# Selective-scan block on one core: B and C spread by DMA, z and output products in array tiles, eight state buffers, and a new order of all steps

## The reference

```
x = x + L0(groupnorm(x))        # nearest of 256 words by cosine, mixed in where close
xn = layernorm(groupnorm(x)) * g + b          # over 256 channels
for each of 4 chunks of 64 channels:          # a "sequence" of 1024 steps
    xi, z = in_proj(chunk)                    # 128 + 128 rows
    xc = silu(causal_conv4(xi) + conv_b)
    dt, B, C = x_proj(xc)                     # 4, 16, 16 rows
    dt = softplus(dt_proj(dt) + dt_proj_b)
    h[d,s] = exp(dt[d]*A[d,s]) * h[d,s] + dt[d]*xc[d]*B[s]    # recurrence over L
    y[d] = sum_s h[d,s]*C[s] + D[d]*xc[d]
    y = out_proj(y * silu(z)) + skip * chunk
x = x + proj(layernorm(all four y))
```

## Time and profile before

| | us |
|---|---|
| three runs: median (lowest, highest) | 5035.2 (5031.6, 5037.42) |
| profiled execution, device time | 5045.31 |
| its span, first to last instruction | 5043.5 |
| busy: PE / DVE / ACT / POOL | 4261.0 / 4235.7 / 2601.2 / 3470.8 |
[...]

### The profile page before, as it was taken

The page is one execution under the profiler, slowest core; times in us unless marked ns, Lnnn a source line. Parts: engine busy times, 40 slices in busy tenths (PEclk is TensorE's granted clock), DMA queues, the critical chain, the costliest instruction groups (busy, mean ns, idle before and its releaser), DMA issues. The chain is left out here.

```text
span 5043.5 us, 50728 instructions
## 1 busy us (share of the span) xinstructions
PE 4261.0 (84%) x13584; PEld 1366.9 (27%) x13584; DVE 4235.7 (84%) x3517; ACT 2601.2 (52%) x3272; POOL 3470.8 (69%) x2101
## 2 busy tenths in 40 slices
PE   3888988888888888988888888888888889888887
PEld 2222323222232222322223232222322223222221
DVE  2688888888888889888888888888888898888886
ACT  2455555554555455455555555555454554555542
POOL 2667767667677766767667676676777667676664
PEclk8798888888898898988888888888988989888887
DMA  1446454554645546455554645546455464555543
GB/s 45 121 131 160 123 141 123 150 145 123 155 117 150 136 128 166 117 142 130 148 150 119 151 112 150 146 125 155 111 152 136 128 166 116 142 130 148 146 129 99
DMA packets 193349, 676.10 MB, mean 134 GB/s; under 512 B 23192, under 2 KB 25056, under 8 KB 189024
## 3 DMA queue, kind: packets, MB, share of 16 engines
q1 hardware_dynamic: 193120, 673.10, 51.7%
HBM read 572.34 MB, written 67.11 MB: 127 GB/s over the span
## 5 line engine op out<-in xcount | busy, mean ns | idle before, releaser
L558 POOL TENSOR_TENSOR state<-state,c_all 128x1024 f32<-128x1024 f32 x1024 | 2411.2, 2358 | 1249.0 <-DVE state L931 1228.6
L931 DVE TENSOR_TENSOR_SCAN state<-dtb,ub 128x1024 f32<-128x1024 f32 x1024 | 2339.2, 2284 | 57.5 <-PE yp L1156 15.0
L1140 PE MATMUL ub<-u,spr 32*128 32x512 f32 x4096 | 1363.2, 747 | 615.7 <-DVE state L931 605.9
L734 ACT ACTIVATE dtb<-dtb,a_neg 128x1024 f32<-128x1024 f32 x1024 | 1164.6, 1142 | 368.0 <-DMA dtb<-dt_scratch 365.9
L922 DVE TENSOR_TENSOR ub<-ub,b_all 128x1024 f32<-128x1024 f32 x1024 | 1242.6, 1213 | 98.4 <-PE ub L1140 63.9
L1140 PEld LDWEIGHTS ub<-u,spr 32*128 32x128 f32 x4096 | 350.7, 209 | 1512.6 <-DVE state L931 1100.6
L1156 PE MATMUL yp<-state,gat 128*32 128x512 f32 x4096 | 627.2, 688 | 4.9 <-POOL state L558 4.9
L1023 PE MATMUL mb<-xs,wtap 128*128 128x512 f32 x512 | 335.2, 814 | 32.7 <-DVE cd L911 22.2
L633 ACT ACTIVATE dt<-mb 128x512 f32<-128x512 f32 x128 | 76.3, 596 | 551.1 <-PE mb L1043 551.1
L822 DVE TENSOR_TENSOR u<-mb,xc 128x512 f32<-128x512 f32 x128 | 88.4, 691 | 289.1 <-ACT dt L633 288.7
L608 ACT ACTIVATE e_x<-mb,ncb 128x512 f32<-128x512 f32 x128 | 87.5, 683 | 260.5 <-PE mb L1023 260.5
(11 more groups left out here) (137 smaller groups left out, 5140.7 us busy)
## 6 DMA issues: line engine op xcount, KB each, us to landing
dtb<-dt_scratch SPq DMA_DIRECT2D x1024, 512.0 KB, 4.7
xs<-xn SPq DMA_DIRECT2D x128, 256.0 KB, 5.7
xt<-in_x SPq DMA_DIRECT2D x16, 1024.0 KB, 7.0
x_scratch<-xt SPq DMA_DIRECT2D x16, 1024.0 KB, 6.8
dt_scratch<-dt SPq DMA_DIRECT2D x64, 256.0 KB, 3.4
dt_scratch<-dt SPq DMA_DIRECT2D x128, 128.0 KB, 3.3
res<-x_scratch SPq DMA_DIRECT2D x16, 1024.0 KB, 10.0
out<-res SPq DMA_DIRECT2D x16, 1024.0 KB, 7.7
```

The lines of the kernel that those rows point to most:

```text
L558: pool.tensor_tensor(v, v, c_all[:, c % 2, :], ALU.mult).then_inc(gated, 1)
L734: act.activation(dtb[:, k, :], dtb[:, k, :], ACT.Exp, scale=a_neg[:, GROUP[g]:GROUP[g] + 1]).then_inc(decayed, 1)
L931: dve.tensor_tensor_scan(state[:, k, :], dtb[:, k, :], ub[:, g % 2, :], 0.0, ALU.mult, ALU.add).then_inc(scanned, 1)
L1140: last = pe.matmul(ub[:, g % 2, h * HALF:(h + 1) * HALF], spr[lo:lo + 32, GROUP[g] % 4, :], u[lo:lo + 32, c % 2, h * HALF:(h + 1) * HALF], ...
```

## The change

B and C are computed as 32 rows (16+16) per half, both halves at once in two column tiles of the array, copied by ACT into `bcs`, stored to DRAM, and fetched by two transfers of 512 KB that repeat each row 8 times. z is computed in its own sequence (not in that before) with its two halves in two row tiles, `post_out` has its halves in two column tiles. `state` has 8 buffers, and a pair is summed in the iteration two later than before. `seq_ready` is gone; PE waits for `prep_u`, DVE and POOL for the two transfers. To make room `yy` is `ll`, `res` is `xn`, `zz` has one buffer. The squares for the pixel norm are no longer added on POOL; PE adds them with twice the one-column matmuls. All slots are new. The input weights are laid out anew on the host (wz, w_bc, w_proj).

```
-LAG = 2
+STATES = 8
+BEHIND = 5
-PE_SEQ = {4: ["prep_xc0"], 5: ["prep_xc1"], 7: ["post_out0"], 8: ["post_out1"], 12: ["prep_raw0"], 13: ["prep_raw1"],
-          18: ["prep_dt0"], 19: ["prep_dt1"], 20: ["prep_b0"], 21: ["prep_b1"], 22: ["prep_c0"], 23: ["prep_c1"],
-          24: ["prep_z0"], 25: ["prep_z1"]}
-ACT_SEQ = {5: ["prep_xc0"], 6: ["prep_xc1"], 8: ["prep_sig_x"], 13: ["prep_raw0"], 14: ["prep_raw1"],
-           15: ["prep_dt_exp", "prep_dt_one"], 16: ["prep_dt_ln"], 19: ["prep_dt0"], 20: ["prep_dt1"],
-           21: ["prep_b0"], 22: ["prep_b1"], 23: ["prep_c0"], 24: ["prep_c1"], 25: ["prep_z0"], 26: ["prep_z1"],
-           27: ["prep_ready"], 30: ["prep_sig_z"]}
-DVE_SEQ = {4: ["post_gate"], 8: ["post_skip0"], 9: ["post_skip1"], 20: ["prep_u0"], 21: ["prep_u1"]}
-POOL_SEQ = {6: ["prep_clamp_x"], 10: ["prep_silu_x"], 16: ["prep_dd"], 28: ["prep_clamp_z"], 31: ["prep_silu_z"]}
-SP_SEQ = {22: ["prep_store"]}
-PE_BATCH = {(0, 9): ["a_group0"], (0, 26): ["a_norm0", "a_norm1", "a_sim00", "a_sim01"], (0, 28): ["a_sim10", "a_sim11"],
-            (0, 29): ["a_sim20", "a_sim21"], (0, 30): ["a_sim30", "a_sim31"],
...
+PE_SEQ = {5: ["prep_xc0", "prep_xc1"], 13: ["prep_raw0"], 14: ["prep_raw1"], 17: ["prep_bc"], 19: ["prep_part0"],
+          20: ["prep_dt0"], 22: ["prep_part1", "prep_dt1"], 24: ["own_z"]}
+ACT_SEQ = {7: ["prep_xc0", "prep_xc1"], 8: ["prep_sig_x"], 15: ["prep_raw0"], 16: ["prep_raw1"],
+           17: ["prep_dt_exp", "prep_dt_one"], 18: ["prep_dt_ln", "prep_bc0"], 19: ["prep_bc1"], 21: ["prep_dt0"],
+           25: ["prep_dt1"], 26: ["own_z0"], 27: ["own_z1", "own_sig_z"]}
+DVE_SEQ = {9: ["post_gate"], 24: ["prep_u0"], 25: ["prep_u1"]}
+POOL_SEQ = {3: ["prep_clamp_x"], 5: ["prep_silu_x"], 16: ["prep_dd"], 24: ["own_clamp_z"], 31: ["own_silu_z"]}
+SP_SEQ = {19: ["prep_bc_store"], 22: ["prep_bc_load"], 23: ["prep_store"]}
+PE_BATCH = {(0, 11): ["a_group0"], (0, 12): ["post_out"], (0, 26): ["a_norm0"], (0, 28): ["a_norm1"],
+            (0, 29): ["a_sim00", "a_sim01", "a_sim10", "a_sim11", "a_sim20", "a_sim21"],
+            (0, 30): ["a_sim30", "a_sim31"], (1, 0): ["c_mean0"], (1, 1): ["c_square0"], (1, 6): ["c_mean1"],
+            (1, 7): ["c_square1"], (1, 8): ["a_turn0"], (1, 11): ["a_turn1"], (1, 12): ["a_keep0", "a_word00"],
+            (1, 13): ["a_word01", "a_keep1", "a_word10", "a_word11"], (1, 15): ["post_out"],
+            (1, 27): ["a_group1", "c_proj00", "c_proj01"], (1, 29): ["c_proj10", "c_proj11"],
+            (2, 0): ["a_mean0", "a_square0"], (2, 6): ["a_mean1"], (2, 7): ["a_square1"], (2, 11): ["post_out"],
+            (3, 10): ["post_out"]}
+DVE_BATCH = {(0, 9): ["a_stat00"], (0, 10): ["a_stat01"], (0, 12): ["a_gm0"], (0, 13): ["post_skip0", "post_skip1"],
+             (0, 31): ["a_pick0", "a_idx0", "a_pick1", "a_idx1", "a_pick2", "a_idx2", "a_pick3", "a_idx3"],
+             (1, 3): ["c_var0", "c_ctr0"], (1, 9): ["c_var1"], (1, 11): ["c_ctr1"], (1, 12): ["a_keep0"],
+             (1, 13): ["a_mix00"], (1, 14): ["a_mix01", "a_keep1"], (1, 15): ["a_mix10", "a_mix11"],
+             (1, 17): ["post_skip0", "post_skip1"], (1, 24): ["a_stat10"], (1, 25): ["a_stat11"], (1, 28): ["a_gm1"],
+             (1, 29): ["c_out00", "c_out01"], (1, 31): ["c_out10", "c_out11"], (2, 3): ["a_var0", "a_ctr0"],
+             (2, 9): ["a_var1", "a_ctr1"], (2, 12): ["post_skip0"], (2, 14): ["post_skip1"],
+             (3, 12): ["post_skip0", "post_skip1"]}
+SP_BATCH = {(0, 4): ["x_in"], (0, 15): ["xs3"], (0, 17): ["x2_back"], (2, 2): ["x2_store"], (2, 6): ["out"],
+            (2, 13): ["xs0"], (2, 17): ["xs1"], (2, 20): ["out_wait"], (3, 15): ["xs2"]}
...
-        state = sb("state", [P, RING, L])
+        state = sb("state", [P, STATES, L])
...
+            def store_bc(m, par):
+
+                await_(bc_copied, 2 * m + 2)
+                for h in range(2):
+                    sp.dma_start(bc_s[par, :, h * HALF:(h + 1) * HALF],
+                                 bcs[32 * h:32 * h + 32, :]).then_inc(s_bcst, 16)
+
+            def load_bc(m, par):
+
+                await_(s_bcst, 32 * (m + 1))
+                await_(bx_done, 16 * (m - 1))
+                await_(gated, 16 * (m - 1))
+                for dst, first, done in ((b_all, 0, s_ball), (c_all, NS, s_call)):
+                    src = bc_s[par, first:first + NS, :].unsqueeze(1).broadcast_to((NS, 8, L))
+                    sp.dma_start(dst[:, par, :], src).then_inc(done, 16)
...
+                elif name == "own_z":
+                    for q in range(2):
+                        bank = enter(kind, b, (f"own_z{q}", c))
+                        lo = DM * q
+                        first = PAD + q + q * HALF
+                        pe.matmul(mb[:, bank, :], wz[lo:lo + DM, :], xs[lo:lo + DM, c, first:first + HALF],
+                                  start=True, stop=True).then_inc(m_full[bank], 1)
...
+                elif name == "prep_bc":
+                    for q in range(2):
+                        bank = enter(kind, b, (f"prep_bc{q}", c))
+                        pe.matmul(mb[32 * q:32 * q + 32, bank, :], wbc[:, q, :], xc[:, par, q * HALF:(q + 1) * HALF],
+                                  start=True, stop=True).then_inc(m_full[bank], 1)
...
                     pe.wait_ge(y_taken, m - 1)
-                    lo = DM * ((c - 1) % 2)
-                    bank = enter(kind, b, (name, c))
-                    pe.matmul(mb[lo:lo + DM, bank, :], wo[:, h, :], yy[:, cut], start=True, stop=True).then_inc(m_full[bank], 1)
+                    for q in range(2):
+                        lo = DM * ((c - 1 + q) % 2)
+                        bank = enter(kind, b, (f"post_out{q}", c))
+                        pe.matmul(mb[lo:lo + DM, bank, :], wo[:, q, :], yy[:, q * HALF:(q + 1) * HALF],
+                                  start=True, stop=True).then_inc(m_full[bank], 1)
...
-                            if g > LAG:
-                                sum_pair(b, c, g - LAG - 1)
+                            if g >= BEHIND:
+                                sum_pair(b, c, g - BEHIND)
```

More of the change, by code:

```diff
@@ L90, in plan @@
     names = []
-    for name in seq_plan.get(j, []):
+    for name in seq_plan.get(j, []) + batch_plan.get((c, j), []):
         if name.startswith("post") and kind == FIRST and c == 0:
@@ L103, in plan @@
     return names
-SINGLE = {"a_group0": 0, "a_norm0": 0, "a_sim00": 1, "a_sim10": 0, "a_sim20": 1, "a_sim30": 0,
-          "a_turn0": 0, "a_turn1": 1, "a_keep0": 0, "a_word00": 1, "a_word01": 0, "a_keep1": 1,
-          "a_word10": 0, "a_word11": 1, "a_group1": 0}
+SINGLE = {"a_group0": 0, "a_norm0": 0, "a_sim00": 1, "a_sim10": 0, "a_sim20": 1, "a_sim30": 0, "a_turn0": 1,
+          "a_turn1": 1, "a_keep0": 0, "a_word00": 1, "a_word01": 0, "a_keep1": 1, "a_word10": 0, "a_word11": 1,
+          "a_group1": 1}
+PAIRED = ("prep_bc", "own_z", "post_out")
 def bank_use(name, c):
+    if name in PAIRED:
+        return [(h, (f"{name}{h}", c)) for h in range(2)]
+    if name.startswith("prep_dt"):
+        return []
+    if name.startswith("prep_part"):
+        return [(int(name[-1]), (f"prep_dt{name[-1]}", c))]
     if name.startswith(("prep", "post")):
@@ L128 @@
          + ["a_" + w for w in STATS])
-PREP_ALL = [f"prep_{w}{h}" for w in ("xc", "raw", "dt", "b", "c", "z") for h in range(2)]
+PREP_ALL = ["prep_xc0", "prep_xc1", "prep_raw0", "prep_raw1", "prep_bc", "prep_part0", "prep_dt0", "prep_part1", "prep_dt1"]
 C_STATS = ["c_" + w for w in STATS]
@@ L143, in __init__ @@
                              for n in plan(PE_SEQ, PE_BATCH, kind, c, j) for u in bank_use(n, c)])
-        self.note("tail", [u for n in ["post_out0", "post_out1"] + C_STATS + C_PROJ for u in bank_use(n, 0)])
+        self.note("tail", [u for n in ["post_out"] + C_STATS + C_PROJ for u in bank_use(n, 0)])
     def note(self, kind, uses):
@@ L403, in do @@
                     await_(s_x2st, 16 * b)
+                    for q in range(NC):
+                        await_(s_xs[q], 32 * (NB if kind == "tail" else b + 1))
                     sp.dma_start(res[:], x2_v[b - 1]).then_inc(s_x2ld, 16)
@@ L685, in do @@
                         act.wait_ge(x2_done, NJ * (t + 1))
-                        at_least(act, s_xs[3], 32 * t)
-                    act.activation((xn if g else cd)[:, j, :], xt[:, j, :], ACT.Square, scale=gsm[:, 4, j:j + 1],
+                        if kind not in ("pro", FIRST):
+                            for q in range(2):
+                                bank, use = banks(kind, b, (f"c_proj1{q}", 0))
+                                act.wait_ge(m_full[bank], use)
+                    act.activation(cd[:, j, :], xt[:, j, :], ACT.Square, scale=gsm[:, 4, j:j + 1],
                                    bias=gsm[:, 5, j:j + 1])
@@ L810, in do @@
                             dve.wait_ge(m_free[mean_bank], mean_use)
-                    start = PAD + q % 2 + h * HALF
+                    start = PAD + (q + h) % 2 + h * HALF
                     dve.scalar_tensor_tensor(
```

(29 more changed lines are left out.)

158 lines of the change are left out of this document (76 added, 82 removed), and 18 rows, old and new, of tables (ACT_BATCH, DVE_BATCH, PE_BATCH).

## The result

| us | before | changed |
|---|---|---|
| median of 4 runs | 5036.31 | 4810.66 (4795.69 to 4819.65) |
| ratio, 95% interval | | 0.9549 (0.952 to 0.9578) |
| profiled execution, its span | 5045.31, 5043.5 | 4817.56, 4815.6 |
| mean granted clock | 0.866 | 0.836 |

The trace's records of the granted clock hold two values in every run here, 1.0 and 0.5; they are called full and half clock, and a mean between them is a mixture in time.

The account below looks back on a forecast made before the run. DVE was taken as the bound, with 808 us of idle to win. Set-up 149.6, image 0 272.4, loop 3934, image 15 254.1 and tail 39.2 gave a 4649 us span, said as 4640 (-7.8%) for the runs; range 4510 to 4860.

Parts of the forecast that it names:

- The bound: DVE's multiply and scan, 3.5 us per unit, set the pace; its 808 us of idle are waits of order.
- u and ym: DVE's waits for ACT's copy of dt and for the output matmul: 15.8 and 8.1 us per image go.
- near 4 us per image: Sign to look for: what stays of u's wait for ACT's dt copy, from PE at half clock.
- The conv: Start of each sequence, at low clock: the spread behind the conv comes late, costing 5.5 us per image.
- sim: Word search at the end of sequence 0: DVE's wait for its matmuls goes, 2.6 us per image.
- at a tenth: Share of PE's saving that the norm's doubled one-column matmuls were set to take back; sum after it about -315 us.
- DVE's own chains and the loop: Idle that stays on DVE: 1.4 us per image in its small chains, 2.4 at the loop's return.
- Keep, norms, projection: Sequence 1's keep and the norm at the start of 2, behind the projection, about 1 us late each: 2 per image.
- PE's work: PE busy time: z -63 us, output -69, B and C -216, less the norm's part; about -315, 20 per image.
- The transfers: Rival: transfers or SP's order become the bound, 2 to 4.5 us per sequence, 4770 to 4930 us; chance 0.13.
- The clock by half or more: Rival about PE's low clock; loop images of 290 us or more would show clock or transfers; chance 0.17.
- The better case: Rival: clock waits stay at 3 us per image, idle is 9, time 4510 us; chance 0.09.

Follow-up runs that it names:

- e3: The change's new parts in the slots of the kernel before, with sums as early as before: 5259 us, ratio 1.0483 to the kernel before.
- e7: Changed kernel with B and C made on PE again by eight full products per sequence, no transfers for them: 4885 us.
- e8: Changed kernel with the halves of z and of the output one after the other, not in tiles, all slots kept: 4802 us, ratio 0.9543.
- e11: e10 with the conv's second half one slot later, so that unit 4's spread comes between the halves: 4727 us, ratio 0.9387.
- e10: Changed kernel with the pixel norm's squares added on POOL again and half the one-column matmuls on PE: 4742 us, ratio 0.9429.
- e12: e11 with the halves of z and of the output one after the other, not in tiles: 4685 us, ratio 0.9304.
- e5: Changed kernel with one added full-array product before each spread in iterations 13, 14, 15, 0 and 1, 20 per image: 4827 us.
- e6: Kernel before the change with 20 added full-array products per image in iterations 13, 14, 15, 0 and 1: 5107 us.
- e2: Changed kernel with spreads issued twice in iterations 13, 14, 15, 0, 1, 3, 4, 6, 7 and 8, 40 more per image: 5060 us.
- e1: Changed kernel with spreads issued twice in iterations 13, 14, 15, 0 and 1, 20 more per image: 4979 us.
- e9: Changed kernel with five added full-array products per image, only around the start of sequence 3: 4810 us.

## Why the prediction was right, and where it was not

**The bound.** Right: in every run the multiply and the scan, 3.5 us per unit, are DVE's; its work stayed (4248 us), its waits were what could be won, and they were of order. e3 shows it sharply: the parts alone, in the old order, are a loss. The order without one of the parts is a gain: e7 has B and C on PE and is still 152 us faster than the kernel before.

**u and ym.** Right that both waits go; u is waited for once more in the whole loop (39.2 - 36.4 = 2.8 us), so the sign "near 4 us per image" did not come. DVE loses time there at the spreads of units 9 to 12 instead: 3.3 us per image in sequence 0, 0.1, 0.5 and 0.5 in the others. These 4.4 where I had kept 4 are luck, not the mechanism: unit 9 (1.1 us in sequence 0) stands behind the products of `prep_raw`, unit 11 (1.9) behind the first dt matmuls, both at half clock in the image shown (0.50 from 2508.3 to 2525.4 us), and in e8, with the dt matmuls as they are, sequence 0 has neither wait. Nor do the rows 6 shown bear out that eight dt matmuls bring the clock up; the trace does in part (mean granted clock 0.50 from 2552 to 2556 us, 0.91 from 2557 to 2566).

**The conv.** 5.5 us per image forecast; the multiply's wait for the spread was 2.2, 0.3, 0.0 and 2.7 for unit 4 of the four sequences, 5.2. "What is late next is the spread behind the conv" holds for the largest part, 5.2 x 14 = 73 of the 170.7 us. e11 takes two thirds of this wait away by its place, and most of the time comes back elsewhere.

**sim.** The step that failed. "2.6 go" was 2.9 and its followers (the multiplies of units 13 and 15, 1.1). I set the norm's doubled matmuls "at a tenth" of the PE sum, 31 us, and asked what they cost PE in total, not where they stand. They took 88.6 us instead of 32.8 and stand straight before the sims. With its followers that is 4.0 us of idle per image where I had none; e10 puts 69 us on this one term, two fifths of the error.

**DVE's own chains and the loop.** Forecast 1.4 + 2.4; measured 3.2 (51 us of waits like best after sim and mv after stats, over 16 images) and 2.9 (40.9 us over 14 images). I had read the chains from three releasers of two lines only: 2.3 per image more together, 37 us, mis-sized.

**Keep, norms, projection.** Forecast 2; gt 2.1, rs (49.4 - 13.3) / 16 = 2.3, the projection (the wait of xn, 16.3 us) 1.0: 5.3, mis-sized by 3.3, 53 us. e7, which puts more before them, doubles gt's. The 11.8 us per image are thus sim 4.0, this 3.3, the chains and the loop 2.3, dt 0.4, conv -0.3, DVE's own work 0.9 (264.9 against 264.0), and 1.2 that I have not placed.

**PE's work.** Counted -315, measured -95. z went from 127.0 to 110.8 us and not to 64, the output from 138.4 to 93.1, B and C from 271 to 86.0; the norm rose by 56. B's products had taken 127.1 us and not C's 143.8 as I took them to, so the count was 17 too large from the start. z's miss is not one of the clock: 57 of its 64 pairs ran at full clock. Where the two products stand together they do overlap, 1.13 us the pair; but the second needs its PSUM bank, which in sequence 1 DVE's u still has to be read from:

```profile
2535.27 1.13 PE L1061 MATMUL mb<-xs,wz 64*128 64x512 f32 x4
...
2621.25 1.12 PE L1061 MATMUL mb<-xs,wz 64*128 64x512 f32 x2
2623.46 1.12 PE L1061 MATMUL mb<-xs,wz 64*128 64x512 f32 x2 [1.09 <-DVE u L851]
```

And work that nobody touched grew: the products with D 128.8 to 170.5, the sums 627.2 to 681.8 and the dt projection 150.7 to 175.4 us, while low time rose from 2 x 0.134 x 5043.5 = 1352 to 2 x 0.164 x 4815.6 = 1579 us. In e12, at a clock of 0.868, those with D took 127.0 again.

**The rivals.** The transfers: no, in this order. The load rose from 134 to 156 GB/s and SP was held for ACT's copies of dt and B, C for 500 us, but a decay was waited for once; e7, without these transfers, is slower. In e3 the same transfers, placed otherwise, hold the scan for 58 us. The clock by half or more: in part. The clock's share in the range's 4860 is my estimate for conv and dt at half clock in every sequence, which no run shows. What the runs showed in its place: the mean clock fell from 0.866 to 0.836, and of DVE's idle time in the loop 46% stands at half clock, which holds 32% of the time (before: 18% and 25%), 12.9 us per image from 7.3. But the clock is not a lever that adds up: e5 raised it to 0.875 and e7 to 0.864 without gain, e12 reached 0.868 with one. More work on PE raised it with full products (e5: 0.875 from 0.836; e6: 0.897 from 0.866) and with the forty doubled spreads of e2 (0.869), and did not with the twenty of e1 (0.831). The better case has a slip: 4650 - 130 is 4520, and its 4510 is counted from 4640.

**What stays open.** Why z and output without tiles win 2.3 to 2.5 us per image in units 6 to 11 of sequence 0, in e8 as in e12. The stretch is known, and that the clock is high behind the output products of that place (units 7 and 8 low for 0 and 0.02 of the time in e8, for 0 and 0 in e12); that in e8 the gain is lost again before the sims is measured. Whether the longer output products hold the clock, or z's, or the phase of the order does, no run separates. Nor does one say what the two transfers would cost without contention.

## What to carry to other kernels

Where one engine sets the pace and another makes its inputs, work taken from the second is worth what the first waits for it at that place: 53 us of tiny matmuls in front of a wait cost 69, while 112 us of products elsewhere cost nothing in e8, and in e12 the kernel was faster with such products than without. A part and the order it needs are one change: measured in the old order, these parts made the kernel 4.8% slower (58 us of it by the placing of the transfers), and in the new one 4.5% faster. Ask of work added to a light engine which step stands right behind it.

## What the runs showed of the hardware

- Twenty more spreads per image (32 rows of the array, two halves at once) left the mean granted clock at 0.831, from 0.836, and forty gave 0.869; twenty products over the full array in the same iterations as the twenty spreads gave 0.875 (changed kernel) and 0.897 (kernel before, from 0.866).
- A step of 16 one-column matmul instructions took 1.95 us at full clock, where four of 512 columns take 1.98. In the image shown it took 2.12 us, and PE's weight loads were busy for 2.10 of them: in the kernel each of these matmuls has weights of its own (512 weight loads for 512 of them). In 13 of the 14 loop images of the changed kernel the mean granted clock of the 4 us behind the first step was 0.50 to 0.72; in e10, with steps of 8, it was 1.0 in 13 of 14.
- Two z products in two row tiles took 1.13 us a pair at full clock where both could start, 0.85 less than two one after the other (1.98). Over the run it was 110.8 / 64 = 1.73 us, against 147.4 / 64 = 2.30 in e8: the second one often waited for its PSUM bank (PE's weight loads stood 38.8 us and its products 16.3 us before z until DVE's u had read it). The output's pairs in two column tiles took 93.1 / 64 = 1.45, against 168.1 / 64 = 2.63, with part of the time at half clock in both.
- Runs of one kernel spread by 0.3 to 0.8% (e9: 4780 to 4817 us), those of e3 by 1.4% (5238 to 5310), and the loop images of one execution of the changed kernel take 286.9 to 297.3 us, of the kernel before 301.1 to 307.2.
